# Decoder layer on one core: another cyclic order of all engines' steps

## The chip, the cores and the metric

The kernel runs on one core of a Trainium2 chip. The metric is the device time of one execution in microseconds (us). A core has TensorE (PE, matmuls; PEld is its weight load), VectorE (DVE), ScalarE (ACT) and GpSimd (POOL), which compute, and SyncE (SP), which here issues the DMAs. Each takes its instructions in a fixed order of its own and waits for others on semaphores.

## The reference

64 sequences of 256 tokens with 256 features each, and a context of 120 tokens per sequence, go through one decoder layer in fp32: local attention (16 heads, each token sees three neighbours to either side), cross attention to the context, causal attention, and a feed-forward block whose output is scaled by a factor from a gate.

```python
x = x + local_attn(_layernorm(x))                # window of 7
x = x + cross_attn(_layernorm(x), ctx_1024)      # 16 heads, 120 keys
x = x + ffn(_layernorm(x))
# ffn(h): h = h + causal_attn(rmsnorm(h, n1_w))
#         xf = rmsnorm(h, n2_w)
#         ef = silu(xf @ up_w.T) @ down_w.T          # 1024 hidden
#         return h + ef * sum(ew)                    # ew: top 2 of the gate's softmax
```

## The kernel before

Each sequence is cut into named steps, and five sequences are in flight at once, each in a lane (a set of buffers; `LANES`, line 14). For one sequence the steps are, in the order of the data:

- `load`; then per layer `moments` (VectorE, GpSimd) and `norm` (ScalarE) for the layernorm, and `turn` (TensorE transposes, L790; ScalarE copies them out, L1028). `turn_ctx` (L797) turns the context.
- Local attention: `project_rows` k, v, q (L810, taken out on VectorE at L1327). SP sends keys and values to DRAM and fetches them back as overlapping windows (`send` L703, `fetch` L719); there is one key window and one value window for all lanes. GpSimd multiplies in twelve chunks (`window_times`: six with keys, L630, six with values, L635), VectorE sums each (`window_reduce`, L1361), with `window_max` (L1370 to L1374), `window_exp` (ScalarE, L1081) and `window_sum` (L1379 to L1382) between the halves. Then `turn_out` (L925) and `project_out` (0) (L939, added on VectorE at L1444).
- Cross (layer 1) and causal (layer 2) attention: `project` (layer, q/k/v) (L832, L838), `max` (layer, part) (masks L860, scores L866; VectorE takes the row maxima, L1407), `shift` (L877; L1411) and `place`, two DMAs that put the maxima beside the queries, `scores` (layer, unit) (L888; ScalarE's exponentials L1075; for the causal layer GpSimd's mask L1232), `values` (L911; `normalise` on VectorE), `project_out` (layer).
- Feed-forward: `turn` (3), `gate` (L950), `up` (0) to (3) (L961; tanh on ScalarE L1108, product on VectorE L1460), `down` (L970; L1469), `store`.

`max` and `scores` use TensorE as four tiles of 32 rows, `values` and `gate` as four tiles of 32 columns; all other steps use the whole array. PSUM has 8 banks: `max` and `scores` take a whole half of four, `values` takes two, the others one. A step may not start before the step that had its bank last has been taken out.

The order is made when the program is built, by `Plan` (line 306). TensorE's order is the sorted list of `n + POSITION[step]`, n being the sequence, so one table gives a cyclic order in which each sequence does the same as the one before it one turn later:

```python
if engine == "PE":
    due[i] = POSITION.get((name, args), 0.0)
else:
    due[i] = min((due[j] for j in followers[i]), default=6.0) + SHIFTED.get((name, args, engine), 0.0)
...
line = sorted((n + due[i], n, i) for n, i in todo if parts[i].engine == "PE")
```

Every other engine takes, of the steps whose inputs are there by the planner's durations, the one due first; a step is due when its earliest follower is, shifted by `SHIFTED`. At the two ends of the run (`FILLING`, `LOOKS`) TensorE may look up to 60 entries ahead for a step that is ready. Where the planner expects TensorE to stand still for more than 1 us (`LONG_WAIT`), it puts dummy bf16 matmuls in front of the next step (`passing`; L770), one for each 0.213 us of expected idle time beyond 0.8 us, twice that while it takes TensorE to be cold. Once, at the start, the weights are loaded and derived; on VectorE these are the biases (L1292, L1296) and the scaling of the causal, up, gate and down weights (L1301 to L1305).

Of the kernel before, what the change touches and what calls it, by code (L numbers as in the profile page):

```python
# [29 lines left out]
ACT = mybir.ActivationFunctionType  # L30
# [28 lines left out]
def score_units(layer):  # L59
# [28 lines left out]
POSITION = {("turn", (0,)): -0.0773, ("turn_ctx", ()): -0.0394, ("project_rows", ("k",)): -0.0389, ("project_rows",  # L88
    ("v",)): 0.0516, ("project_rows", ("q",)): 0.0643, ("project", (1, "v")): 0.8052, ("turn_out", ()): 1.0641,
    ("project_out", (0,)): 1.2473, ("project", (1, "k")): 1.2641, ("turn", (1,)): 1.4729, ("project", (1, "q")):  # L90
    1.5195, ("max", (1, 0)): 1.6554, ("max", (1, 1)): 1.6713, ("shift", (1,)): 1.8861, ("scores", (1, 1)): 1.9724,
    ("scores", (1, 0)): 2.0874, ("values", (1,)): 2.3718, ("project_out", (1,)): 2.5298, ("turn", (2,)): 2.6364,
    ("project", (2, "k")): 2.7808, ("project", (2, "q")): 2.8094, ("max", (2, 0)): 2.8523, ("project", (2, "v")):
    2.899, ("max", (2, 1)): 3.0514, ("max", (2, 2)): 3.1338, ("shift", (2,)): 3.2929, ("scores", (2, 1)): 3.4513,
    ("scores", (2, 0)): 3.53, ("scores", (2, 2)): 3.6057, ("values", (2,)): 3.8413, ("project_out", (2,)): 3.9289,
    ("turn", (3,)): 4.2641, ("up", (0,)): 4.3625, ("up", (1,)): 4.3677, ("gate", ()): 4.4232, ("up", (2,)): 4.4727,
    ("up", (3,)): 4.4907, ("down", ()): 4.6197}
# [208 lines left out]
class Plan:  # L306
# [3 lines left out]
    def __init__(self, N, T, C):  # L310
# [14 lines left out]
        for i in reversed(range(len(parts))):  # L325
            name, args, engine = parts[i][:3]
# [4 lines that stand above are left out]
        engines = ("PE", "ACT", "DVE", "POOL", "SP")  # L331
# [1182 lines left out]
```

How the kernel before makes its waits and increments, by code:

```python
        def once(eng, known, what, signal, count):  # L649
            if what not in known:
                known.add(what)
                eng.wait_ge(signal, count)
# [1 line left out]
        def wait_taken(eng, name, n, *args):  # L655
            for b, used in fills[name, n, args]:
                eng.wait_ge(emptied[b], used + 1)
# [2 lines left out]
            @block.sync  # L661
# [19 lines left out]
                                dst = W[what] if dst is None else dst[:, :, 0:E] if what == "gate" else dst  # L681
                                sp.dma_start(dst if what in staged or what == "gate" else dst[:],
                                             src.rearrange("(k p) n -> p k n", p=P)).then_inc(loaded[n], 16)
                    elif name == "zeros":
                        sp.wait_ge(filled_ones, 1)
                        for first in (0, T + HALO):
                            dst = passed_on[:, first:first + HALO, :].rearrange("a r d -> r a d")
# [1 line left out]
                            sp.dma_start(dst, src).then_inc(zeroed, 16)  # L690
                    elif name == "load":
                        before = plan.before["lane", seq, ()]
                        if before:
                            sp.wait_ge(stored[s], reached["stored", "store", before[0], ()])
                        sp.dma_start(x[s][:], t["x"][seq].rearrange("(b p) d -> p b d", p=P)).then_inc(x_loaded[s], 16)
                        sp.dma_start(cx[s][0:C, :], t["ctx_1024"][seq]).then_inc(ctx_loaded[s], 16)
```

## Time and profile before

| | |
|---|---|
| time, median of 3 runs | 3522.82 us (3520.79 to 3526.21) |
| profiled execution, its own time | 3523.18 us |
| its span, first to last instruction | 3521.5 us |
| granted TensorE clock | 0.999 of full |
| TensorE, matmuls | 3464.6 us busy, 98%, 36557 instructions |
| TensorE, weight loads | 2788.9 us, 79% |
| VectorE | 2674.4 us, 76% |
| ScalarE | 1828.8 us, 52% |
| GpSimd | 2498.7 us, 71% |
| DMA | 223.35 MB, mean 63 GB/s |

The busy shares are means over the whole span. Where one engine is near 100% over a stretch, the length of that stretch is read from its own instructions and their starts; where it is not, from what it waits for. TensorE's instructions overlap, so the length of a step is read from start to start and not from its duration. A dummy matmul counts as busy.

### The profile page before, as it was taken

What the parts mean: (1) busy time and instruction counts of PE and PEld (TensorE: products, weight loads), DVE (VectorE), ACT (ScalarE), POOL (GpSimd) and SP (SyncE); (2) the same over time, 40 slices, a digit from 0 to 9 for tenths busy, and PEclk for the clock granted to TensorE, in tenths of its full rate; (3) what the DMA queues carried; (4) which work ended last, traced back from release to release, by engine and by line L of the source; (5) the groups of instructions that cost most, each with busy time, mean ns of one, the idle gap of its engine ahead of it and who ended that gap; (6) DMA issues with size and microseconds to landing.
All of it is one profiled execution on the core that took longest, in us unless ns stands there. A gap on an engine that the chain in (4) does not pass through costs nothing.

```text
span 3521.5 us, 92506 instructions
## 1 busy us (share of the span) xinstructions
PE 3464.6 (98%) x36557; PEld 2788.9 (79%) x36557; DVE 2674.4 (76%) x5867; ACT 1828.8 (52%) x4241; POOL 2498.7 (71%) x3160
## 2 busy tenths in 40 slices
PE   8899999999999999999999999999999999999998
PEld 5577888888888888888888888888888888888876
DVE  5677787787787787787787787787787787787763
ACT  3344555555555555555545545545545545545542
POOL 5767777777777777777777777777777777777731
PEclk9999999999999999999999999999999999999999
DMA  5111221121121121221121221221221121121200
GB/s 182 50 51 50 70 73 51 68 74 51 68 74 52 67 74 50 69 74 50 66 77 47 69 77 46 69 77 47 69 77 47 69 77 47 69 77 47 69 8 10
DMA packets 90151, 223.35 MB, mean 63 GB/s; under 512 B 9286, under 2 KB 56706, under 8 KB 73346
## 3 DMA queue, kind: packets, MB, share of 16 engines
q1 hardware_dynamic: 89730, 217.44, 18.1%
q8 instruction: 300, 4.92, 0.6%
q14 instruction: 121, 0.99, 0.1%
HBM read 164.92 MB, written 50.39 MB: 61 GB/s over the span
## 4 chain that ended last, share of the span: by engine, by line
PE 94%; POOL 2%; ACT 2%; DVE 2%; issue 1%; SPq 0%; DMA 0%; DVEq 0%; POOLq 0%; ACTq 0%
PE ps L970 13%; PE ps L961 13%; PE ps L832 11%; PE ps L810 10%; PE ps L888 9%; PE ps L939 9%; PE ps L866 9%; PE ps L911 8%; PE ps L838 5%; PE ps L790 3%; PE ps L860 1%; PE ps L877 1%; ACT prob L1075 1%; PE ps L925 1%; POOL chunks L635 1%; DVE nmax L1407 1%
## 5 line engine op out<-in xcount | busy, mean ns | idle before, releaser
L635 POOL TENSOR_TENSOR chunks<-v_windows,xT 128x560 f32<-128x560 f32 (+1 forms) x384 | 879.6, 2301 | 92.2 <-DVE xT L1382 89.2
L1407 DVE TENSOR_REDUCE nmax<-ps 128x4 f32<-128x480 f32 (+2 forms) x1280 | 776.9, 671 | 182.8 <-PE ps L866 182.6
L1075 ACT ACTIVATE prob<-ps 128x256 f32<-128x256 f32 (+2 forms) x1536 | 670.7, 556 | 457.7 <-PE ps L888 457.5
L630 POOL TENSOR_TENSOR chunks<-rest,k_windows 128x512 f32<-128x512 f32 (+1 forms) x384 | 552.2, 1455 | 373.9 <-DMA k_windows<-passed_on 301.1
L1361 DVE TENSOR_REDUCE held<-chunks 128x80 f32<-128x560 f32 (+1 forms) x384 | 294.6, 768 | 321.2 <-POOL chunks L635 319.8
L961 PE MATMUL ps<-xT,w_up 128*128 128x256 f32 x2048 | 480.3, 383 | 1.4 <-ACT xT L1028 1.3
L970 PE MATMUL ps<-w_down,held 128*128 128x256 f32 x2048 | 459.1, 382 | 1.1 <-DVE held L1460 1.0
L970 PEld LDWEIGHTS ps<-w_down,held 128*128 128x128 f32 x2048 | 383.8, 190 | 60.1 <-DVE held L1460 2.8
L961 PEld LDWEIGHTS ps<-xT,w_up 128*128 128x128 f32 x2048 | 372.4, 190 | 69.4 <-issue 20.6
L1232 POOL TENSOR_SCALAR_AFFINE_SELECT prob<-prob 128x512 f32<-128x512 f32 x512 | 311.3, 642 | 50.6 <-ACT prob L1075 50.6
L1028 ACT COPY xT<-ps 128x512 f32<-128x512 f32 x256 | 152.9, 597 | 361.6 <-PE ps L790 361.6
L1361 DVE TENSOR_REDUCE xT<-chunks 128x32 f32<-128x512 f32 (+1 forms) x384 | 291.9, 760 | 21.8 <-POOL chunks L630 21.7
L911 PE MATMUL ps<-prob,va 120*32 120x256 f32 (+2 forms) x6144 | 303.5, 346 | 4.2 <-ACT prob L1075 2.0
L911 PEld LDWEIGHTS ps<-prob,va 120*32 120x32 f32 (+1 forms) x6144 | 179.7, 110 | 122.4 <-issue 45.9
L866 PE MATMUL ps<-held 32*128 32x120 f32 (+2 forms) x4096 | 260.2, 321 | 3.2 <-ACT held L1045 2.4
L888 PE MATMUL ps<-held 32*128 32x128 f32 (+2 forms) x3072 | 241.4, 380 | 10.0 <-issue 4.6
L1204 POOL TENSOR_TENSOR x<-x,y 128x512 f32<-128x512 f32 x64 | 81.4, 1272 | 233.8 <-DVE y L1444 233.8
L1016 ACT ACTIVATE held<-x,nmean,rstd 128x256 f32<-128x256 f32 x256 | 140.0, 595 | 186.0 <-POOL nmean L1179 186.0
L1108 ACT ACTIVATE rest<-ps 128x512 f32<-128x512 f32 x256 | 154.7, 604 | 115.9 <-PE ps L961 115.9
L888 PEld LDWEIGHTS ps<-held 32*128 32x128 f32 (+1 forms) x3072 | 123.1, 181 | 97.2 <-issue 90.1
L1460 DVE SCALAR_TENSOR_TENSOR held<-rest,ps 128x512 f32<-128x512 f32 x256 | 172.7, 675 | 23.1 <-ACT rest L1108 22.4
L1418 DVE STREAM_TRANSPOSE ps<-ps 128x512 f32<-128x512 f32 x256 | 170.1, 707 | 20.0 <-PE ps L911 19.3
(152 smaller groups left out, 6783.8 us busy)
## 6 DMA issues: line engine op xcount, KB each, us to landing
k_windows<-passed_on SPq DMA_DIRECT2D x64, 1024.0 KB, 5.0
v_windows<-passed_on SPq DMA_DIRECT2D x64, 1024.0 KB, 5.0
x<-in_x SPq DMA_DIRECT2D x64, 256.0 KB, 2.9
passed_on<-rest SPq DMA_DIRECT2D x64, 256.0 KB, 2.3
passed_on<-held SPq DMA_DIRECT2D x64, 256.0 KB, 3.7
out<-x SPq DMA_DIRECT2D x64, 256.0 KB, 2.2
y<-in_ctx SPq DMA_DIRECT2D x64, 120.0 KB, 2.9
held<-nmaxT SPq DMA_DIRECT2D x256, 8.0 KB
```

The costliest lines, as they stand in the source:

```text
L630: return engine.tensor_tensor(chunk_of(c).rearrange("p (j d) -> p j d", d=D), token_rows["q"][s][:, b, :].unsqueeze(1).to_broadcast([P, n, ...
L635: return engine.tensor_tensor(chunk_of(c).rearrange("p (h i j) -> p h i j", i=HD, j=WINDOW), window("v", b * D + first * HD, (HD, n), (1, ...
L810: last = nc.tensor.matmul(ps[:, b, tb * D:(tb + 1) * D], tokens, W[f"local_{w}"][:, k, :], start=(k == 0), stop=(k == 1))
L832: last = nc.tensor.matmul(ps[:, b, m * n:(m + 1) * n], wt[:, k, m * P:(m + 1) * P], src[:, k, 0:n], start=(k == 0), stop=(k == 1))
L866: last = nc.tensor.matmul(ps[:, to[r], place * keys:(place + 1) * keys], qT[s][e][rows, m, tb * P:(tb + 1) * P], kT[L][s][e][rows, m, 0:keys],
L888: last = nc.tensor.matmul(ps[0:keys, to[r], n * qs:(n + 1) * qs], kT[L][s][e][rows, m, key0:key0 + keys], qT[s][e][rows, m, q0:q0 + qs], s ...
L911: last = nc.tensor.matmul(ps[SLOT * j:SLOT * (j + 1), b, e * T + q0:e * T + q0 + qs], va[s][0:keys, kb, head:head + SLOT], pr[0:keys, j, c ...
L961: last = nc.tensor.matmul(ps[:, b, m * T:(m + 1) * T], w_up[:, k, (2 * m2 + m) * P:(2 * m2 + m + 1) * P], xT[s][:, k, :], start=(k == 0), ...
L970: last = nc.tensor.matmul(ps[:, b, tb * D:(tb + 1) * D], hid[s][:, m, tb * P:(tb + 1) * P], w_down[:, m, :], start=(m == 0), stop=(m == F ...
L1075: last = nc.scalar.activation(prob_pair(seq, L, m)[0:keys, :, r, col:col + qs], of_pair, ACT.Exp, scale=SCALE)
L1361: nc.vector.tensor_reduce(to, chunk_of(c).rearrange("p (x i) -> p x i", i=width), AX_X, ALU.add).then_inc(reduced[s], 1)
L1407: nc.vector.tensor_reduce(of_heads[:, ms[0]:ms[-1] + 1, :, r], src, AX_X, ALU.max, negate=True).then_inc(emptied[b], 1)
```

## The change

The numbers in `POSITION` and `SHIFTED` are others; all else is the same. The number of steps on each engine and all their instructions are the same but for the dummies: 328 before, 248 now. Two entries of the diff:

```diff
-POSITION = {("turn", (0,)): -0.0773, ("turn_ctx", ()): -0.0394, ("project_rows", ("k",)): -0.0389, ("project_rows",
...
+POSITION = {("turn", (0,)): 0.9219, ("turn_ctx", ()): 0.9774, ("project_rows", ("k",)): 0.9776, ("project_rows",
...
-SHIFTED = {("down", (), "DVE"): -0.0629, ("fetch", ("k",), "SP"): 0.2, ("fetch", ("v",), "SP"): 0.5928, ("gate", (),
...
+SHIFTED = {("down", (), "DVE"): 0.325, ("fetch", ("k",), "SP"): -0.274, ("gate", (), "ACT"): 0.1684, ("max", (1, 0),
...
```

TensorE's order over one cycle in the middle of the run, with the sequence that each step belongs to. Before: turn_ctx 30, project_rows k 30, scores (1,1) 28, max (2,1) 27, project_rows v 30, turn_out 29, project_rows q 30, scores (1,0) 28, max (2,2) 27, project_out (0) 29, turn (3) 26, project (1,k) 29, shift (2) 27, up (0) 26, up (1) 26, values (1) 28, gate 26, scores (2,1) 27, up (2) 26, turn (1) 29, up (3) 26, project (1,q) 29, project_out (1) 28, scores (2,0) 27, scores (2,2) 27, down 26, turn (2) 28, max (1,0) 29, max (1,1) 29, project (2,k) 28, project (1,v) 30, project (2,q) 28, values (2) 27, max (2,0) 28, shift (1) 29, project (2,v) 28, turn (0) 31, project_out (2) 27.

Now: turn_ctx 30, project_out (2) 26, project_rows k 30, scores (1,0) 28, max (2,1) 27, project (1,v) 28, turn_out 29, project_rows v 30, max (2,2) 27, scores (1,1) 28, project_rows q 30, shift (2) 27, project_out (0) 29, turn (3) 26, values (1) 28, gate 26, scores (2,1) 27, up (0) 26, up (1) 26, up (2) 26, project_out (1) 28, turn (1) 29, scores (2,0) 27, up (3) 26, project (1,q) 29, down 26, turn (2) 28, scores (2,2) 27, max (1,0) 29, project (2,q) 28, project (2,k) 28, max (1,1) 29, project (1,k) 30, values (2) 27, max (2,0) 28, shift (1) 29, project (2,v) 28, turn (0) 31.

The first place: TensorE from `down` on (L790 is `turn`, L866 `max` (1), L888 with 128x128 `scores` (2,2), L832 and L838 projections, L911 `values` (2)). Before:

```order
L970 MATMUL ps<-w_down,held 128x256 x16
L790 MATMUL ps<-ident,held 128x128 x4
L866 MATMUL ps<-held 128x120 x4
L866 MATMUL ps<-y,held 128x120 x4
...
L832 MATMUL ps<-xT,w_causal_k 128x256 x4
L838 MATMUL ps<-w_cross_v,y 120x256 x2
L832 MATMUL ps<-xT,w_causal_q 128x256 x4
L911 MATMUL ps<-prob,va 32x256 x4
```

Now:

```order
L970 MATMUL ps<-w_down,held 128x256 x16
L790 MATMUL ps<-ident,held 128x128 x4
L888 MATMUL ps<-held 128x128 x4
L888 MATMUL ps<-held,rest 128x128 x4
...
L866 MATMUL ps<-held 128x120 x4
L866 MATMUL ps<-y,held 128x120 x4
...
L832 MATMUL ps<-xT,w_causal_q 128x256 x4
L832 MATMUL ps<-xT,w_causal_k 128x256 x4
L866 MATMUL ps<-held 128x120 x4
L866 MATMUL ps<-y,held 128x120 x4
...
L832 MATMUL ps<-y,w_cross_k 128x120 x4
L911 MATMUL ps<-prob,va 32x256 x4
```

The two `max` (1) steps, 32 matmuls in one run before, are apart, the second between two projections, and the causal `scores` (2,2) stands ahead of the first.

The second place: VectorE in the first sequence, from its fifth window reduce on. Before:

```order
L1361 TENSOR_REDUCE xT<-chunks 128x32
L1398 TENSOR_TENSOR va<-ps,b_cross_v 120x16x16
L1301 TENSOR_SCALAR w_causal_v<-w_causal_v,scale 128x256
...
L1305 TENSOR_SCALAR w_down<-w_down 128x2048
L1361 TENSOR_REDUCE xT<-chunks 128x32
L1327 TENSOR_TENSOR rest<-ps,b_local_q 128x512
L1370 TENSOR_TENSOR xT<-xT,edge_mask 128x224
```

Now:

```order
L1361 TENSOR_REDUCE xT<-chunks 128x32
L1327 TENSOR_TENSOR held<-ps,b_local_v 128x512
L1370 TENSOR_TENSOR xT<-xT,edge_mask 128x224
...
L1382 TENSOR_TENSOR xT<-xT,rsum 128x224
L1301 TENSOR_SCALAR w_causal_v<-w_causal_v,scale 128x256
...
L1305 TENSOR_SCALAR w_down<-w_down 128x2048
L1361 TENSOR_REDUCE held<-chunks 128x96
```

The scaling of the weights has moved from ahead of `window_max` to behind `window_sum`.

The third place: TensorE ahead of the first `turn_out` (L925). Before:

```order
L832 MATMUL ps<-y,w_cross_k 128x120 x4
L810 MATMUL ps<-w_local_q,xT 128x256 x4
L770 MATMUL ps<-ident_b 128x512 x73
L925 MATMUL ps<-ident,held 128x128 x4
L939 MATMUL ps<-w_local_o,xT 128x256 x4
```

Now:

```order
L832 MATMUL ps<-y,w_cross_k 128x120 x4
L838 MATMUL ps<-w_cross_v,y 120x256 x2
L810 MATMUL ps<-w_local_v,xT 128x256 x4
L810 MATMUL ps<-w_local_q,xT 128x256 x4
L770 MATMUL ps<-ident_b 128x512 x61
L925 MATMUL ps<-ident,held 128x128 x4
L939 MATMUL ps<-w_local_o,xT 128x256 x4
```

The dummies are 61 in place of 73, and the last cross-key projection (L832) stands three steps ahead of them where it stood one step ahead. Three earlier places with 10, 4 and 4 dummies, ahead of TensorE's first steps, are gone.

## Rows read from the trace of the kernel before

**Rows 1.** The page: busy us and share of each engine; shares of the chain.
```profile
PE 3464.6 (98%) x36557; PEld 2788.9 (79%) x36557; DVE 2674.4 (76%) x5867; ACT 1828.8 (52%) x4241; POOL 2498.7 (71%) x3160
...
PE 94%; POOL 2%; ACT 2%; DVE 2%; issue 1%; SPq 0%; DMA 0%; DVEq 0%; POOLq 0%; ACTq 0%
```

**Rows 2.** Busy time by stretch: stretch, length, each engine's busy us (instructions), clock, DMA.
```profile
232.00:3147.00 2915.00, 2904.05 (x31126) 2367.55 (x31124) 2284.37 (x5005) 1564.84 (x3626) 2143.00 (x2693) 1.00 0.19 64
```

**Rows 3.** The chain in order of time: start us, us, what.
```profile
2017.18 7.10 PE ps L970 x32
2069.92 7.10 PE ps L970 x32
```

**Rows 4.** TensorE's timeline inside one cycle: start us, us, instructions.
```profile
1677.81 0.30 PE L860 MATMUL ps<-mask_rows,pick_rows 32*128 32x64 bf16 x16 [0.19 <-issue]
...
1687.99 0.71 PE L888 MATMUL ps<-held 32*128 32x256 f32 x8
...
1689.07 1.99 PE L961 MATMUL ps<-xT,w_up 128*128 128x256 f32 x8
1690.90 0.60 PE L790 MATMUL ps<-ident,held 128*128 128x128 f32 x4
...
1693.07 1.89 PE L832 MATMUL ps<-xT,w_cross_q 128*128 128x256 f32 x8
1694.79 1.89 PE L939 MATMUL ps<-w_cross_o,xT 128*128 128x256 f32 x8
1696.61 0.71 PE L888 MATMUL ps<-held 32*128 32x256 f32 x8
...
1697.65 0.50 PE L888 MATMUL ps<-held 32*128 32x128 f32 x8
```

**Rows 5.** Waits, 430 to 3147 us: who waited for whom, us, times, longest.
```profile
POOL chunks L630 <- DMA k_windows<-passed_on: 258.0, 49, 7.3
...
PEld ps L911 <- issue: 34.1, 103, 0.3
```

**Rows 6.** The dummy matmuls of L770 alone, by stretch: PE busy (count) first.
```profile
0.00:72.00 72.00, 23.32 (x91) 9.36 (x91) 0.98 0.60 194
72.00:232.00 160.00, 35.66 (x152) 14.23 (x152) 1.00 0.15 51
...
3434.00:3522.00 88.00, 15.90 (x69) 6.50 (x69) 0.98 0.03 10
```

**Rows 7.** TensorE's timeline, 54 to 84 us.
```profile
55.49 15.92 PE L770 MATMUL ps<-ident_b 128*128 128x512 bf16 x73
71.40 0.66 PE L925 MATMUL ps<-ident,held 128*128 128x128 f32 x4
```

**Rows 8.** GpSimd's timeline, 55 to 76 us.
```profile
57.25 13.32 POOL L635 TENSOR_TENSOR chunks<-v_windows,xT 128x672 f32<-128x672 f32 x6 [11.05 <-DVE xT L1382]
```

**Rows 9.** The timelines of VectorE and of ScalarE, 44 to 58 us.
```profile
46.28 0.34 DVE L1301 TENSOR_SCALAR w_causal_v<-w_causal_v,scale 128x256 f32<-128x256 f32 x1
...
48.42 1.22 DVE L1305 TENSOR_SCALAR w_down<-w_down 128x2048 f32<-128x2048 f32 x1
...
50.75 0.38 DVE L1370 TENSOR_TENSOR xT<-xT,edge_mask 128x224 f32<-128x224 f32 x1
...
55.31 0.40 ACT L1081 ACTIVATE xT<-xT 128x224 f32<-128x224 f32 x1
```

**Rows 10.** Waits of TensorE over the whole run.
```profile
PE ps L970 <- DVE held L1460: 1.0, 2, 0.6
```

**Rows 11.** The timelines of ScalarE and of VectorE inside one cycle.
```profile
1689.21 2.06 ACT L1075 ACTIVATE prob<-ps 128x512 f32<-128x512 f32 x4 [0.86 <-PE ps L888]
1691.14 0.63 ACT L1108 ACTIVATE rest<-ps 128x512 f32<-128x512 f32 x1
...
1693.96 0.69 DVE L1460 SCALAR_TENSOR_TENSOR held<-rest,ps 128x512 f32<-128x512 f32 x1
```

**Rows 12.** TensorE's timeline, 228 to 244 us.
```profile
231.62 0.60 PE L790 MATMUL ps<-ident,held 128*128 128x128 f32 x4
```

More of the change, by code:

```diff
@@ L86 @@
 BEHIND = {("weights", (3,), "SP"): ("fetch", ("k",), "SP", 0), ("weights", (4,), "SP"): ("fetch", ("v",), "SP", 0)}
-POSITION = {("turn", (0,)): -0.0773, ("turn_ctx", ()): -0.0394, ("project_rows", ("k",)): -0.0389, ("project_rows",
[L89 to L97, printed above, removed]
@@ new lines @@
+POSITION = {("turn", (0,)): 0.9219, ("turn_ctx", ()): 0.9774, ("project_rows", ("k",)): 0.9776, ("project_rows",
+    ("v",)): 1.1332, ("project_rows", ("q",)): 1.1518, ("project", (1, "k")): 1.8134, ("turn_out", ()): 2.0879,
+    ("project_out", (0,)): 2.1783, ("turn", (1,)): 2.2808, ("project", (1, "q")): 2.4795, ("max", (1, 0)): 2.7336,
+    ("max", (1, 1)): 2.7883, ("shift", (1,)): 2.9153, ("scores", (1, 0)): 3.0592, ("project", (1, "v")): 3.0877,
+    ("scores", (1, 1)): 3.1516, ("values", (1,)): 3.1832, ("project_out", (1,)): 3.2808, ("turn", (2,)): 3.6475,
+    ("project", (2, "q")): 3.7881, ("project", (2, "k")): 3.7881, ("max", (2, 0)): 3.9003, ("project", (2, "v")):
+    3.9219, ("max", (2, 1)): 4.0874, ("max", (2, 2)): 4.1511, ("shift", (2,)): 4.1766, ("scores", (2, 1)): 4.2144,
+    ("scores", (2, 0)): 4.4344, ("scores", (2, 2)): 4.6983, ("values", (2,)): 4.8138, ("project_out", (2,)): 4.9776,
+    ("turn", (3,)): 5.1785, ("gate", ()): 5.1834, ("up", (0,)): 5.2155, ("up", (1,)): 5.2297, ("up", (2,)): 5.2301,
+    ("up", (3,)): 5.4346, ("down", ()): 5.4797}
```

50 lines of the change are left out of this document (25 added, 25 removed).

## The prediction

> **What bounds the kernel now.** I read the page's busy shares and its chain first. TensorE is busy 3464.6 of 3521.5 us (98%), VectorE 76%, GpSimd 71%, ScalarE 52%, and TensorE holds 94% of the chain that ended last [rows 1]. So time counts where TensorE works longer or waits. The busy sums by stretch come next: from 232 to 3147 us it is busy 2904 of 2915 us [rows 2], so its empty time lies in the filling before and in the drain behind. In the chain, `down` of one sequence starts at 2017.18 and of the next at 2069.92 [rows 3]: one cycle is some 52.7 us. Two levers follow: the length of a cycle, paid about 57 times, and the empty time at the two ends, paid once.
>
> TensorE's timeline shows what order costs inside a cycle [rows 4]. A projection with whole-array neighbours goes from start to start in 1.72 us (1693.07 to 1694.79). The same work right ahead of a group of 32-row tiles takes 1.82 (1694.79 to 1696.61), right behind such a group 1.83 (1689.07 to 1690.90). I call a run of `max`, `scores`, `values` and `gate` steps between whole-array steps a spell. A spell costs its neighbours 0.10 each, 0.20 together, and its own last step 0.04 more: `scores` takes 1.04 with another `scores` behind it (1696.61 to 1697.65) and 1.08 with `up` behind it (1687.99 to 1689.07). The waits list has the same from the weight loader: 103 pauses ahead of L911 with 34.1 us together, 0.33 each [rows 5], two a cycle.
>
> The empty time shows in the dummy matmuls of L770, which stand where the planner expects TensorE to wait for over 1 us: 91 of them before 72 us, 152 from there to 232 us, 69 behind 3434 us [rows 6]. Of the 73 ahead of sequence 0's `turn_out` one takes 15.92/73 = 0.218 us [rows 7].
>
> **The change part by part.** No instruction changes its form, tile or size; the positions and the orders that hang on them do.
>
> *1. Spells.* Before, a cycle has six: scores/max, scores/max, values/gate/scores, scores/scores, max/max, values/max. Changed, `scores` (2,0) stands alone between `turn` and `up`, `scores` (2,2) has joined `max` (1,0), and `max` (1,1) stands alone between two projections: seven. Counted over the whole orders, 398 spells become 455, 57 more. At 0.20 + 0.04 = 0.24 us each that is **+13.7 us**, all on TensorE, where nothing hides it. Lower end: the neighbours alone at 0.19, +10.8. Upper end: a spell that also shows a pause such as the 0.19 us ahead of L860 at 1677.81 [rows 4], 0.43, +24. I take 0.24, a difference of like rows.
>
> The Trainium skill (TensorEngine Tiling, Key Properties) says that a change of the tiling mode drains the array. Its page TensorE: Matmul & The Clock Gate (Single matmul latency) puts a drain at about 175 ns; by that, an estimate, the 114 added switches would cost 20 us. The trace shows such a cost on both sides of a spell, but 0.10 each.
>
> *2. The first sequence.* GpSimd starts the value half of sequence 0 at 57.25, after 11.05 us without work, on the end of VectorE's softmax sum [rows 8]. On VectorE the scaling of the weights, 46.28 to 49.64, stands ahead of L1370 at 50.75; on ScalarE the exponential (L1081) at 55.31 stands behind four evictions of cross keys [rows 9], the last fed by the projection two steps ahead of the dummies. The change puts the scaling behind the softmax sum, so L1370 comes 3.3 us earlier, and the feeding projection four steps ahead of the dummies, two more projections earlier. GpSimd's six products end at 57.25 + 13.32 = 70.57 [rows 8] and `turn_out` starts at 71.40 [rows 7]; sequence 1's products queue behind them, so what is won here shifts the whole filling. I take **-5.0 us**. The 12 dummies fewer in front of `turn_out`, 61 for 73, say 2.6 of it, with projections drawn forward; the 18 dummies that the first 30 us lose stood in waits for loads, which stay, and count nothing. Ends: -1.7 (the exponential moves by one projection) and -6.7 (scaling, and two projections). Against it stands that SP fetches sequence 0's keys behind two more sends; no row prices that, and it lies inside these ends.
>
> *3. The rest of the filling.* From `project_out` of sequence 0 to `turn` of sequence 5 there are 119 dummies for 152 [rows 6]. 33 x 0.218 = **-7.2 us**, if the planner's expectation is as good as for the 73, whose last ended when `turn_out` could start. Ends -3 and -10.
>
> *4. The drain.* The last four places (19, 11, 19, 4) are alike. Ahead of them 27 dummies become 15: at 15.90/69 = 0.23 [rows 6] **-2.8 us**; ends 0 and -4.
>
> *5. Waits in the cycle.* Now GpSimd waits 258.0 us in 49 pauses for the key window [rows 5], and its jitter comes through to TensorE's `scores` and `max` groups. In the changed order seven steps in place of four stand between the key and the query projection, so the keys are there when the queries come and GpSimd starts on the queries: I take off 0.2 us a cycle. Against that, `project` (2,q) takes the first bank of `scores` (2,2) 0.9 us after that step, where it stood behind ScalarE's first two of eight activations, and `turn_out` a bank of `max` (2,1) 1 us behind it: 0.1 each, 0.25 with smaller ones, from distances between starts. Net 0.05 x 57 = **+3 us**; ends -10 (the gain alone) and +14 (the loss alone).
>
> Sum: 13.7 - 5.0 - 7.2 - 2.8 + 3 = +1.7 on the profiled execution's own 3523.18: 3524.9, rounded to **3525 us**. The median before, 3522.82, lies 0.4 below that execution. A measurement of this kernel tells about 0.2% (7 us) from no change; the forecast is inside.
>
> **The rivals.**
>
> *A. The ends win (faster).* Parts 2 to 4 come out at their good ends, -6.7 - 10 - 4 = -20.7, spells at +10.8, and of part 5 half the gain, -5: 3523.2 - 14.9 = **3508**. For it: fewer dummies in three separate places. Against it: it needs all of them.
>
> *B. `down` waits for `up` (3) (slower).* Now a cross-query projection, `project_out` (1) and two `scores` lie between them, and L970 waited for L1460 only twice [rows 10]. Changed, only the projection is left. From the end of the lone `scores` (2,0) to `down` TensorE has `up` (3) and that projection, 1.83 + 1.72 = 3.55 us; in them ScalarE has four exponentials, 2.06, and the tanh, 0.63, and VectorE the product, 0.69 [rows 11]: 3.38. The slack is 0.17 us, and the case decides from there; VectorE's window softmax (L1370 to L1374) stands right ahead of that product and can use it up. 0.5 us late is 57 x 0.5 = 28 us, **3553**. Against it: each piece fits, just.
>
> *C. A switch costs more than its like rows say.* If an added switch costs TensorE half of the weight loader's pause [rows 5], 0.17, and not 0.12, then 114 x 0.17 = 19 stand in place of 13.7: **3531**, at the edge of slower. The Trainium skill's two pages named above would have it so; the trace agrees that a switch costs something and shows less of it.
>
> *D. The switches cost nothing more,* since TensorE would wait there for its banks anyway: parts 2 to 5 alone, 3523.2 - 12 = **3511**. Rows 4 speak against it. It goes with A.
>
> **How the numbers follow.** The forecast, 3516 to 3530, has 0.38. Faster: A and D 0.33. Slower: B 0.14, C 0.08, other new waits of part 5's kind 0.07, together 0.29. The range takes in A and a little below, and reaches to B: 3503 to 3552. The likeliest case's own is 3516 to 3530.
>
> **What would show it.** (1) `down` every 52.9 to 53.2 us in the middle of the run; at 52.7 or less part 1 is wrong, over 53.4 B or part 5 is. (2) The `up` behind the lone `scores` (2,0), and the projections around the lone `max` (1,1), 0.1 us longer than with whole-array neighbours. (3) `turn_out` of sequence 0 at 65 to 67 us and `turn` of sequence 5 near 219, now 231.62 [rows 12]. (4) For B, a wait of L970 for L1460 in every cycle. (5) GpSimd's wait for the key window mostly gone, one for the query rows in its place. The wrong sign in (3), or a cycle over 53.4, makes the prediction wrong.

## The result, and the profile after

The changed kernel takes **3559.27 us**, median of 4 runs (3554.51 to 3565.55), against 3524.11 (3520.79 to 3526.21) for the kernel before beside it: ratio 1.0102, 95% interval 1.0090 to 1.0114, so 35 us slower. The prediction said 3525 within 3503 to 3552; the result lies outside. The profiled execution took 3554.51, at the low end of the four, with a span of 3552.8.

The page of the changed kernel, its busy times and its chain:

```profile
PE 3458.9 (97%) x36477; PEld 2781.3 (78%) x36477; DVE 2740.6 (77%) x5867; ACT 1815.3 (51%) x4241; POOL 2502.5 (70%) x3160
...
PE 85%; DMA 7%; DVE 2%; POOL 2%; ACT 1%; issue 1%; SPq 1%; DVEq 0%; POOLq 0%; ACTq 0%
```

TensorE has 94% of the chain in [rows 1] and 85% here; DMA, at 0% before, has 7%. The busy times by stretch, first the stretch of [rows 2], then the dummies of L770 alone in the first stretch of [rows 6]:

```profile
232.00:3147.00 2915.00, 2876.98 (x30772) 2337.10 (x30771) 2316.50 (x4943) 1532.47 (x3578) 2116.44 (x2656) 1.00 0.19 64
...
0.00:72.00 72.00, 11.74 (x42) 4.80 (x43) 0.93 0.66 204
```

TensorE is empty for 38 us of the 2915 in which it was empty for 11. So the loss is in the cycle and not at the ends. The starts of `down` in the three traces say how much of it; the third column is the first experiment below.

| | before | changed | placing first |
|---|---|---|---|
| `down` of sequence 3 starts | 375.3 | 372.3 | 366.4 |
| `down` of sequence 58 starts | 3286.0 | 3317.9 | 3282.0 |
| mean cycle between them (55) | 52.92 | 53.56 | 53.01 |
| shortest cycle | 52.7 | 52.8 | 52.8 |
| from there to the end of the span | 235.5 | 234.9 | 235.0 |
| span | 3521.5 | 3552.8 | 3517.0 |

The filling gained 3 us, the drain half a us, and 55 cycles lost 0.63 each, 35. The shortest cycle hardly grew: most of the loss comes in some cycles and not in others. The waits from 430 to 3147 us, as in [rows 5], name the reason:

```profile
POOL chunks L630 <- DVE rest L1327: 328.5, 47, 7.1
...
PE ps L888 <- DMA held<-nmaxT: 31.0, 35, 2.3
```

The last row is new. `scores` waits for the two DMAs of `place`, which put the row maxima beside the queries; over the whole run TensorE waits 36.4 us for them, 39 times. The chain of one such cycle, in order of time:

```profile
2171.75 4.56 DMA passed_on<-held
2176.33 0.32 SPq L719
2176.70 0.54 SPq L728
2177.28 3.99 DMA held<-nmaxT
2181.32 1.15 PE ps L888 x16
```

Read upwards: causal `scores` (2,1) starts at 2181.32, when the maxima have landed. SP issued them at 2176.70 (L728), right behind the 1 MB fetch of the value windows (L719). The fetch had waited for the send of the value rows, on its way since 2171.75. The times of issue in the kernel before, and what a fetch takes from issue to landing, the median on the page of before:

```profile
1677.99 0.32 SPq L719 DMA_DIRECT2D v_windows<-passed_on  x1
...
1683.94 1.10 SPq L728 DMA_DIRECT2D held<-nmaxT  x2
...
v_windows<-passed_on SPq DMA_DIRECT2D x64, 1024.0 KB, 5.0
```

Changed, VectorE's eviction of the maxima and TensorE around the same place:

```profile
2175.66 0.40 DVE L1411 COPY nmaxT<-ps 16x256 f32<-16x256 f32 x1
...
2179.16 0.41 PE L950 MATMUL ps<-xT,w_gate 128*32 128x64 f32 x16
2181.32 0.71 PE L888 MATMUL ps<-held 32*128 32x256 f32 x8 [1.74 <-DMA held<-nmaxT]
```

Before, the fetch left 5.95 us ahead of the placing, so it was over by the median of 5.0, and `scores` began 4.05 us behind the placing (1687.99 in [rows 4]) without a wait. Changed, the fetch leaves 0.37 us ahead of it, since `project_rows` v, whose result SP sends and fetches back, stands four steps ahead of `shift` (2) where it stood eight (5.84 us from start to start, 9.75 before); and TensorE wants the maxima sooner, since only `project_out`, `turn`, `values` and `gate` are left between `shift` and `scores`. Over sequences 8 to 57 the fetch leads by 3.2 to 6.0 us before and by 0.36 to 2.32 changed. Sorted by that lead, the time from placing to `scores` in the changed kernel is:

| lead of the fetch, us | cycles | placing to `scores`, mean (least to most) |
|---|---|---|
| 0.36 | 9 | 4.61 (4.36 to 5.05) |
| 0.5 to 1 | 7 | 4.42 (3.90 to 5.27) |
| 1 to 1.5 | 20 | 3.84 (3.42 to 4.47) |
| 1.5 to 2.32 | 14 | 3.49 (3.42 to 4.05) |

3.42 is what TensorE's own steps take, the case without a wait. In the first rows lead and time add up to nearly the same. In the 29 of these 50 cycles in which `scores` waits for over 0.3 us, it starts 5.12 us behind the issue of the fetch in the mean (4.72 to 6.11), whatever the lead, and the fetch itself takes 5.0 in the median: the placing, small as it is, lands about when the 1 MB does. What inside the transfers makes it so, no run here shows. An estimate from these numbers: there is hardly a wait where the fetch leads by 5.1 - 3.4 = 1.7 us or more.

### The profile page after: what moved, and what is told of

It reads as the page before. It is cut to its first block, busy times and chain, and to the rows that moved or that the text cites. A ratio compares the mean times of both kernels' runs of the same rounds, so it can differ in the third digit from the quotient of the medians.

```text
span 3552.8 us, 92347 instructions
## 1 busy us (share of the span) xinstructions
PE 3458.9 (97%) x36477; PEld 2781.3 (78%) x36477; DVE 2740.6 (77%) x5867; ACT 1815.3 (51%) x4241; POOL 2502.5 (70%) x3160
## 4 chain that ended last, share of the span: by engine, by line
PE 85%; DMA 7%; DVE 2%; POOL 2%; ACT 1%; issue 1%; SPq 1%; DVEq 0%; POOLq 0%; ACTq 0%
PE ps L961 13%; PE ps L970 12%; PE ps L832 11%; PE ps L888 9%; PE ps L810 9%; PE ps L866 8%; PE ps L939 7%; PE ps L911 6%; PE ps L838 5%; DMA held<-nmaxT 4%; PE ps L790 2%; DMA passed_on<-held 1%; PE ps L860 1%; PE ps L770 1%; DVE nmax L1407 1%
## 5 line engine op out<-in xcount | busy, mean ns | idle before, releaser
L635 POOL TENSOR_TENSOR chunks<-v_windows,xT 128x560 f32<-128x560 f32 (+1 forms) x384 | 872.0, 2295 | 31.0 <-DVE xT L1382 25.5
L1028 ACT COPY xT<-ps 128x512 f32<-128x512 f32 x256 | 150.2, 587 | 658.2 <-PE ps L790 658.2
L961 PEld LDWEIGHTS ps<-xT,w_up 128*128 128x128 f32 x2048 | 380.0, 191 | 90.5 <-issue 41.2
L911 PE MATMUL ps<-prob,va 120*32 120x256 f32 (+2 forms) x6144 | 303.5, 346 | 1.5 <-POOL prob L1232 0.9
L888 PE MATMUL ps<-held 32*128 32x128 f32 (+2 forms) x3072 | 236.2, 377 | 39.7 <-DMA held<-nmaxT 36.4
L866 PE MATMUL ps<-held 32*128 32x120 f32 (+2 forms) x4096 | 254.9, 318 | 1.7 <-ACT held L1045 1.6
L911 PEld LDWEIGHTS ps<-prob,va 120*32 120x32 f32 (+1 forms) x6144 | 180.0, 110 | 96.3 <-issue 13.8
L888 PEld LDWEIGHTS ps<-held 32*128 32x128 f32 (+1 forms) x3072 | 121.0, 181 | 103.2 <-issue 49.6
L1316 DVE BATCH_NORM_STATS2 stats<-x 128x6 f32<-128x256 f32 x384 | 143.8, 416 | 68.4 <-DMA x<-in_x 66.3
L866 PEld LDWEIGHTS ps<-held 32*128 32x128 f32 x4096 | 163.5, 186 | 23.8 <-issue 22.1
```

The lines of the kernel that those rows point to most:

```text
L635: return engine.tensor_tensor(chunk_of(c).rearrange("p (h i j) -> p h i j", i=HD, j=WINDOW), window("v", b * D + first * HD, (HD, n), (1, ...
L866: last = nc.tensor.matmul(ps[:, to[r], place * keys:(place + 1) * keys], qT[s][e][rows, m, tb * P:(tb + 1) * P], kT[L][s][e][rows, m, 0:keys],
L888: last = nc.tensor.matmul(ps[0:keys, to[r], n * qs:(n + 1) * qs], kT[L][s][e][rows, m, key0:key0 + keys], qT[s][e][rows, m, q0:q0 + qs], s ...
L911: last = nc.tensor.matmul(ps[SLOT * j:SLOT * (j + 1), b, e * T + q0:e * T + q0 + qs], va[s][0:keys, kb, head:head + SLOT], pr[0:keys, j, c ...
L961: last = nc.tensor.matmul(ps[:, b, m * T:(m + 1) * T], w_up[:, k, (2 * m2 + m) * P:(2 * m2 + m + 1) * P], xT[s][:, k, :], start=(k == 0), ...
```

## The experiments

Theory P: the placing is late because it is issued behind the 1 MB fetch. Rivals: L, its latency alone is too long for the new order; S, the added spells are the loss; and for the filling, D and G on the dummies. Each edit is made after the orders are planned, unless a position is changed. The kernel before ran beside each (3522.53, 3523.52 and 3523.92 us in the three groups).

**1. The placing ahead of the fetch in SP's queue.**

```diff
+        sp = self.order["SP"]
+        for j in range(len(sp) - 1):
+            if sp[j][0] == "fetch" and sp[j][2] == ("v",) and sp[j + 1][0] == "place" and sp[j + 1][2] == (CAUSAL,):
+                sp[j:j + 2] = sp[j + 1], sp[j]
```

> The changed kernel with one exchange in SP's queue: wherever the fetch of the value windows (1 MB) stands right ahead of the placing of the causal maxima, place (2), the placing now goes first. Everything else keeps its order. Theory P (placing behind the fetch): TensorE's wait of scores (2,1) for nmaxT, 36 us over the run and some 29 us by the stretched distance gate to scores, comes from the placing's transfer standing behind the 1 MB fetch issued 0.36 to 2.3 us before it. Then this wait goes (under 5 us in all) and the time is 3527 to 3534, take 3530. Theory L (the placing's own latency is too long for the 4.2 us that the changed TensorE order leaves): the wait stays and the time is 3553 to 3560. Theory S (the 57 added spells are the loss, as part 1 of the prediction priced them at 13.7 us, and more): at most 10 us better, 3549 to 3559.

Measured: **3516.70 us** (3514.99 to 3518.75), ratio to before 0.998 (0.9971 to 0.9989). SP's queue and TensorE in one cycle (L723, L732 and L892 are L719, L728 and L888 of the changed kernel), and the busy times of the stretch:

```profile
2152.23 1.10 SPq L732 DMA_DIRECT2D held<-nmaxT  x2
2153.43 0.38 SPq L723 DMA_DIRECT2D v_windows<-passed_on  x1
...
2155.65 0.71 PE L892 MATMUL ps<-held 32*128 32x256 f32 x8
...
232.00:3147.00 2915.00, 2911.17 (x31124) 2367.92 (x31124) 2331.46 (x5003) 1554.29 (x3630) 2140.72 (x2695) 1.00 0.19 64
```

The wait for the maxima has left the waits list, and TensorE is empty for 4 us of the stretch. P holds; L and S fall: the same TensorE order, with the same latency and all its spells, is 43 us faster than the changed kernel by the medians (36 by the profiled spans, the changed kernel's being its fastest run) and 5.8 us faster than the kernel before. The gain is above the 29 us expected, and the time 10 us under the range given for P. By the profiled spans the 36 us gained are the 36.4 us of waiting; the expectation had counted 29 of them. That the changed kernel's other runs, 3 to 11 us longer, wait more is likely but not shown, since only one of them has a trace.

**2. The kernel before, its fetch held back until the maxima are ready.**

```diff
+                        if w == "v" and later and later[0][0] == "place" and later[0][2] == (CAUSAL,):
+                            wait_taken(sp, "shift", later[0][1], CAUSAL)
```

> The kernel before, with its own TensorE order and six spells a cycle; SP now holds the fetch of the value windows back until the causal maxima are ready to be placed, so that the fetch leaves some 0.4 us ahead of place (2) and not 3.2 to 6.0 us. Theory P: the placing lands 4.5 to 5.3 us after its issue as in the changed kernel, while TensorE leaves it 4.05 us: 0.5 to 1.3 us of waiting a cycle at scores (2,1), a wait of L888 for nmaxT of 30 to 70 us appears that the kernel before did not have, and the time is 3550 to 3595, take 3570. Theory L: 4.05 us are enough for the placing whatever stands before it, no such wait, 3520 to 3532 (a few us for a later fetch). Should GpSimd come to wait for v_windows instead, the later fetch is the cause and not the placing; the waits list tells.

Measured: **3597.04 us** (3592.31 to 3598.72), ratio 1.0213 (1.0196 to 1.0230), 74.5 us slower. The wait over the run (L891 is L888):

```profile
PE ps L891 <- DMA held<-nmaxT: 63.7, 58, 2.6
```

The lead is 0.36 us in every cycle, and `scores` starts 4.31 to 5.31 us behind the placing in every cycle, mean 4.71, as in the first line of the table, or 5.07 behind the fetch. The wait appears in the old order, in 58 pauses. P holds; the time is 2 us above the range given. GpSimd waits once, 9.5 us, for the value windows, in the filling; that belongs to the later fetch itself.

**3. The fetch in halves, one ahead of the placing and one behind.**

```diff
-                        sp.dma_start(windows[w][:], ...)
+                            half_fetch(s, 0)
+                            if later and later[0][0] == "place" and later[0][2] == (CAUSAL,):
+                                held_back.append(s)
+                            else:
+                                half_fetch(s, 1)
```

> The changed kernel with each value fetch in two transfers of 512 KB; where place (2) follows, the first half goes ahead of it and the second behind it. Theory P with the bytes ahead as what counts: the placing waits for about half as long, which the slack of about 0.6 us between 3.4 and 4.0 us largely covers; the wait of scores (2,1) falls from 36 us to 3 to 15 us, time 3532 to 3545. Theory P with the mere presence of a large transfer ahead as what counts: the wait stays near 30 us, 3553 to 3562. Theory L: no change, 3555 to 3562.

Measured: 3521.78 us (3519.10 to 3524.45), ratio 0.9999 (0.9990 to 1.0009). Over the run (L907 is L888):

```profile
PE ps L907 <- DMA held<-nmaxT: 9.9, 16, 1.2
```

Half the bytes ahead leave 9.9 of 36.4 us of waiting, as P expects where bytes count; 5 us over experiment 1, below the range of 3532 to 3545, which had been laid too high with the same 29 us. In the cycles that wait, `scores` starts 3.85 us behind the half fetch, for 5.12 behind the whole one. This kernel still has the placing behind a fetch that waits for its send; so that blocking, without the second half, costs at most these 9.9 us.

**4. Fewer dummies ahead of the first `turn_out`.**

```diff
+        self.passing["turn_out", 0, ()] -= 28
```

> The changed kernel with 33 dummy matmuls ahead of turn_out of sequence 0 in place of 61, nothing else changed. In the changed kernel they start at 60.26 us, behind 7.6 us without work, and end at 76.3, though the last reduce that turn_out waits for is done by about 69. So turn_out should start at 69 to 70 us. Theory D (the dummies delay the filling as a whole): everything behind comes 6 to 7 us earlier, 3552. Theory G (GpSimd, whose products of sequence 1 began at 69.2 regardless, sets the filling): turn (3) of sequence 1 and down of sequence 0 move by less than 3 us, time 3556 to 3560.

Measured: **3567.08 us** (3564.83 to 3571.37), 8 slower than the changed kernel. The filling did what it should: `turn_out` of sequence 0 starts at 68.96 for 76.16, and `down` of sequence 0 at 203.6 for 208.8. That is 5.2 of the 6 to 7 us of D at the start; G, under 3 us there, falls. At `down` of sequence 3, 369.0 for 372.3, 3.3 us are left. From there to `down` of 58 a cycle takes 53.92 us in place of 53.56. TensorE waits 48.8 us for the maxima (36.4), and the granted clock fell more often. The fetch leads by only 0.36 us in 15 of the 50 cycles of the table, where it was 9: the start of the run has a say in which cycles that happens. Both theories gave a time that leaves the cycles as they were, 3552 and 3556 to 3560, and both missed; the loss in the cycles was in neither.

**5. One spell more in the kernel before.**

```diff
-    ("project_out", (0,)): 1.2473, ... ("max", (1, 0)): 1.6554, ("max", (1, 1)): 1.6713,
+    ("project_out", (0,)): 1.2473, ... ("max", (1, 0)): 1.6280, ("max", (1, 1)): 1.6713,
```

> The kernel before with one step moved: max (1,0) stands ahead of turn (2) and not behind it, so max (1,0) and max (1,1) are two spells; 398 spells become 456, 58 more, and the order is otherwise the same. This prices a spell by itself. Theory S24 (part 1 of the prediction, 0.24 us a spell on TensorE with nothing to hide it): 58 x 0.24 = 14 us, 3536 against 3522.5. Theory S9 (with the placing out of the way the changed order's cycle was 53.01 us against 52.92, so that the added spell costs 0.09): 5 us, 3528. If the step's new place makes a wait for banks or for xT of turn (2), the waits list shows it.

Measured: **3590.55 us** (3589.22 to 3592.53), ratio 1.0191 (1.0177 to 1.0205): a miss for both. The waits from 430 to 3147 us, and ScalarE and TensorE behind one `down`:

```profile
PE ps L866 <- DVE nmax L1407: 50.7, 51, 1.2
...
2386.63 0.59 ACT L1028 COPY xT<-ps 128x512 f32<-128x512 f32 x1 [3.61 <-PE ps L790]
...
2387.58 0.50 PE L866 MATMUL ps<-held 32*128 32x120 f32 x8 [0.98 <-DVE nmax L1407]
```

`max` (1,1) now waits 1.0 us in every cycle. The list puts that down to VectorE's maxima, but by the kernel's plan the four banks of `max` (1,1) were last those of `down`, `turn` (2) and `scores` (2,0), none of them of a `max`. `turn` (2) now stands right ahead of `max` (1,1), without `max` (1,0) between, and ScalarE takes it out from 2386.63 to 2387.22 (L1028); `max` (1,1) starts 0.36 us behind that, as it starts 0.35 us behind the same copy in the kernel before. So the wait is for ScalarE's copy. The mean cycle is 54.08 for 52.92: 1.16, of which 1.0 is this wait. The experiment prices a bank wait, and leaves some 0.2 for the spell.

**6. The changed kernel with `scores` (2,1) one step later.**

```diff
-    ("scores", (2, 1)): 4.2144
+    ("scores", (2, 1)): 4.2200
```

> The changed kernel with SP's queue as it was, the 1 MB fetch ahead of place (2), but scores (2,1) one step later on TensorE: behind up (0) and not behind gate. The placing then has 1.8 us more, some 5.2 us from its issue. Price: scores (2,1) is a spell of its own, 59 more. Theory P (the placing lands 4.3 to 5.3 us after its issue behind the fetch, and only lateness counts): the wait of L888 for nmaxT is nearly gone (under 5 us), and the time is that of the run with the placing first, 3516.7, plus 59 spells: 3522 at 0.09, 3531 at 0.24. Rival (the fetch's traffic slows more than this one wait): 3540 or more with the wait gone.

Measured: **3611.49 us** (3609.36 to 3612.34), ratio 1.0250 (1.0236 to 1.0264). TensorE's waits, 430 to 3147 us:

```profile
PE ps L970 <- DVE held L1460: 38.9, 49, 0.9
```

The wait for the maxima is gone (0.2 us), as P says, and in its place `down` waits for `up` (3) in 49 of some 51 cycles: rival B of the prediction, which did not show in the changed kernel (0.6 us in one pause). The planner also moved ScalarE's and VectorE's steps with this edit, and the cycle is 54.5 us. P's 3522 to 3531 were far too low. The time is where the rival put it, 3540 or more with the wait gone, but the new wait is on VectorE and not on the fetch's traffic, so that the experiment says nothing for the rival. It is shown that B's slack is thin, not how much of the 52 us over the changed kernel is B's.

**7. The two `max` (1) together again, placing first.**

```diff
-    ("max", (1, 1)): 2.7883
+    ("max", (1, 1)): 2.7340
```

> The placing first, and max (1,1) back beside max (1,0): 396 spells as before the change (398). Theory S24: 59 spells fewer, 14 us off 3516.7, 3503. Theory S9: 5 us off, 3511. Rival B2 (the spell was split because three groups of four banks in a row, scores (2,2), max (1,0), max (1,1), must wait for ScalarE's eight activations): TensorE waits 0.5 to 1.5 us a cycle ahead of max (1,1), L866 waits for ScalarE's prob, 3540 to 3600.

Measured: **3598.52 us** (3597.00 to 3599.28), ratio 1.0213 (1.0199 to 1.0227), 82 over experiment 1. TensorE between `max` (1,0) and `max` (1,1), L870:

```profile
2394.12 0.82 PE L774 MATMUL ps<-ident_b 128*128 128x512 bf16 x3
2395.62 0.50 PE L870 MATMUL ps<-held 32*128 32x120 f32 x8 [0.67 <-ACT prob L1079]
```

From 2394.12 to 2395.62 TensorE does nothing of use: the third group of four banks in a row waits for ScalarE's exponentials. B2 holds, at the top of its range. The spell that I booked as a pure cost of the change buys these 1.5 us (net 1.25: the mean cycle is 54.26 here and 53.01 in experiment 1).

**8. Placing first and 33 dummies.** Edits 1 and 4 together.

> The placing first and 33 dummy matmuls ahead of turn_out of sequence 0 in place of 61. With 33 and the fetch first, down of sequence 3 came 3.3 us earlier (369.0 for 372.3) but the whole took 8 us longer, with 12 us more waiting for nmaxT and six stretches of lower granted clock. Theory D2 (the start gains 3 to 4 us, and the loss behind it was all in waits for the placing): 3512 to 3514. Rival (fewer dummies cost something else later): 3517 or more.

Measured: **3515.08 us** (3512.61 to 3517.83), ratio to before 0.9977 (0.9967 to 0.9986), the fastest of all, though 1.6 from experiment 1 is within what the runs scatter. TensorE's start (L775 is L770):

```profile
59.02 8.95 PE L775 MATMUL ps<-ident_b 128*128 128x512 bf16 x33 [7.67 <-DVE rest L1332]
```

`turn_out` starts at 68.10, and no wait for the maxima is left. `down` of sequence 3 starts at 359.6 for 366.4, 6.9 earlier; the span ends 3.6 earlier, since a cycle here takes 53.07 us for 53.01. The start gained more than the 3 to 4 us of D2, the end less: the time lies between the ranges of D2 (up to 3514) and of its rival (from 3517) and decides for neither.

**9. `gate` as a spell of its own, placing first.**

```diff
-    ("gate", ()): 5.1834
+    ("gate", ()): 5.2200
```

> The changed kernel with the placing first, and gate one step later, behind up (0): values and scores (2,1) stay together, gate is a spell of its own, 514 spells for 455. It takes one bank only and its followers on VectorE and ScalarE are short, so that no new wait for banks is expected. Theory S24 (a spell costs 0.24 us): 59 x 0.24 = 14 us over 3516.7, 3531. Theory S9: 59 x 0.09 = 5 us, 3522. Rival (scores (2,1) now comes 0.4 us sooner after the placing and waits): a wait of L888 for nmaxT shows, 3535 or more.

Measured: **3538.06 us** (3534.98 to 3539.63), ratio 1.0039 (1.0027 to 1.0052), 21 over experiment 1. TensorE has no wait for the maxima (its weight loader 1.4 us) and no other new wait. TensorE's timeline, from `values` to behind `up` (L965), where experiment 1 has the three `up` together:

```profile
2324.98 1.93 PE L915 MATMUL ps<-prob,va 120*32 120x256 f32 x32
...
2327.92 1.99 PE L965 MATMUL ps<-xT,w_up 128*128 128x256 f32 x8
2329.84 0.43 PE L954 MATMUL ps<-xT,w_gate 128*32 128x64 f32 x16
2330.20 3.72 PE L965 MATMUL ps<-xT,w_up 128*128 128x256 f32 x16
2333.76 1.89 PE L943 MATMUL ps<-w_cross_o,xT 128*128 128x256 f32 x8
```

Experiment 1 for comparison:

```profile
2153.56 1.93 PE L915 MATMUL ps<-prob,va 120*32 120x256 f32 x32
...
2156.72 5.45 PE L965 MATMUL ps<-xT,w_up 128*128 128x256 f32 x24
2162.01 1.89 PE L943 MATMUL ps<-w_cross_o,xT 128*128 128x256 f32 x8
```

`gate` and the three `up` take 0.34 + 5.29 = 5.63 in experiment 1 and 1.92 + 0.36 + 3.56 = 5.84 here: the added spell costs 0.21 us. `values` and `scores` take 2.94 from 2324.98 to 2327.92, where `values`, `gate` and `scores` take 3.16 from 2153.56 to 2156.72 there: less `gate`'s 0.34 that is 2.82, so 0.12 more where a step in row tiles and not one in column tiles follows. Together 0.33, and the cycle is 53.32 for 53.01. S9 is wrong. S24 is nearer, but the spell costs 0.31 to 0.33 us for its 0.24, and its 3531 was 7 us short. An added spell is two added switches of the tiling, 0.16 us each here.

**10. The placing issued from ScalarE's DMA queue.** The fetch leaves SP at the same place as in the changed kernel.

```diff
+        for step in [step for step in self.order["SP"] if step[0] == "place" and step[2] == (CAUSAL,)]:
+            self.order["SP"].remove(step)
+            shift = at_pe["shift", step[1], (CAUSAL,)]
+            act.insert(next((j for j, a in enumerate(act) if at_pe.get(a, -1) > shift), len(act)), step)
```

> The changed kernel with every place (2) issued from ScalarE's DMA queue in place of SP's, at the same moment in the cycle; the 1 MB fetch leaves SP as before. Theory Q (what delays the placing is its place behind the fetch in the same queue): the wait of scores (2,1) for nmaxT falls under 5 us, 3515 to 3522. Theory E (the engines and the memory are shared, whichever queue issues): the wait stays at 20 to 36 us, 3540 to 3560. Both should lose SP's own blocking, where the fetch waits for its send and the placing behind it. ScalarE may pay for the issues: if its waits grow, the time is higher with the wait for nmaxT gone.

Measured: 3554.63 us (3552.14 to 3563.59), ratio 1.0093 (1.0078 to 1.0107). One cycle (L725 the fetch, L1036 the placing, L894 `scores`), and the wait over the run:

```profile
2173.23 0.32 SPq L725 DMA_DIRECT2D v_windows<-passed_on  x1
...
2174.48 1.12 ACTq L1036 DMA_DIRECT2D held<-nmaxT  x2
...
2179.01 0.71 PE L894 MATMUL ps<-held 32*128 32x256 f32 x8 [1.05 <-DMA held<-nmaxT]
...
PE ps L894 <- DMA held<-nmaxT: 35.6, 39, 2.1
```

35.6 us for 36.4: another queue helps nothing. At the same lead the time from placing to `scores` is the same too, 4.32 for 4.42 at 0.5 to 1 us and 3.81 for 3.84 at 1 to 1.5. In 5 of the 50 cycles the first of the two DMAs leaves 0.12 to 0.62 us ahead of the fetch, and `scores` still starts 5.1 to 5.6 us behind it; in experiment 1, where both are issued before the fetch, it is 3.42. Theory E holds, and SP's own blocking, gone here, was worth about 1 us of waiting and at most 5 us of time.

The Trainium skill (DMA: Bandwidth & Descriptors, Issuing engines are not separate DMA queues) says that transfers started by different engines run on the same 16 DMA engines and interleave; the trace agrees, with 35.6 against 36.4 us. The same page of the Trainium skill (Queues, rings and completion order) says that each DMA engine takes turns between the queues, packet by packet. From that one might infer that the 8 KB of a placing in a queue of its own pass the 1 MB; the skill does not say so, and no such gain shows here.

**12. The kernel before with the exchange of experiment 1.** (There is no 11.)

> The kernel before with the same exchange in SP's queue as brought the changed kernel from 3559 to 3517: place (2) ahead of the fetch of the value windows. Here TensorE never waited for nmaxT, so theory P expects nothing: 3519 to 3526, or a loss where the fetch, now some 4.5 us later, makes GpSimd wait for v_windows. Rival (a later fetch is good for something else, such as the other transfers): 3510 to 3517, as in the changed kernel, whose gain over the kernel before would then come from the exchange and not from the order.

Measured: 3532.21 us (3529.18 to 3535.07), ratio 1.0022 (1.0012 to 1.0032), 8.3 slower. Waits over the run (L639 is L635):

```profile
POOL chunks L639 <- DMA v_windows<-passed_on: 11.1, 1, 11.1
```

The cycle is unchanged, 52.96 for 52.92. The loss is in the filling: GpSimd waits for one late fetch until 210.4, TensorE stands still for 4.6 us until 214.4, its granted clock is 0.50 for the 6.8 us from 213.7 on, and `down` of sequence 3 starts at 384.6 for 375.3. So the exchange is no gain by itself, and the 5.8 us by which experiment 1 beats the kernel before belong to the changed order.

## Why the prediction was wrong

Its sum was 1.7 us over the profiled execution of before; with the placing out of the way the changed order comes to 3517.0 - 3521.5 = 4.5 us under it in span. The step that failed is the count of what the change moves: **SP's queue and the DMAs were never part of it**. Part 5, *Waits in the cycle*, looked for what comes late next among banks, GpSimd and ScalarE, and of SP the whole prediction names only the fetch of sequence 0's keys, in part 2. The order of SP's steps in a cycle is the same in both kernels, and that was taken for no change; what changed is the time between them. Rows for it were at hand before: a fetch 3.2 to 6.0 us ahead of a placing, and `scores` 4.05 us behind. The order shows the value rows moved four steps towards `shift` (2), and TensorE's steps from `shift` to `scores` cut. That a placing lands about with the fetch ahead of it, the price of the collision, stood in no row of before. The result also fails two of the prediction's own signs: a cycle over 53.4 us (53.56), and the sign of (3) at `turn_out`.

Part by part:

- *1, spells, +13.7.* Right in mechanism, and in price where it can be read most plainly, around the lone `scores` (2,0) of the changed kernel:

```profile
2189.40 0.60 PE L790 MATMUL ps<-ident,held 128*128 128x128 f32 x4
2189.93 0.71 PE L888 MATMUL ps<-held 32*128 32x256 f32 x8
...
2191.01 1.99 PE L961 MATMUL ps<-xT,w_up 128*128 128x256 f32 x8
2192.84 1.89 PE L832 MATMUL ps<-xT,w_cross_q 128*128 128x256 f32 x8
```

  `turn` takes 0.53 from start to start for 0.44 ([rows 4], 1690.90 to 1691.34), `scores` 1.08 for 1.04, `up` (3) 1.83 and the projection behind it 1.73 for 1.72: 0.24 in all, as predicted. But not all spells are alike. The lone `gate` of experiment 9 costs 0.33, of which 0.12 is `values` with `scores` behind it and not `gate`; and the lone `max` (1,1) saves 1.2 us a cycle of waiting for banks (54.26 in experiment 7, 53.01 in experiment 1).
- *2, the first sequence, -5.0.* Wrong sign on the profiled execution: `turn_out` at 76.16 for 71.40, where 65 to 67 was predicted. GpSimd's value half does start 5.6 us earlier, at 51.66 for 57.25 [rows 8]. Three things undo it. The first two, in the timelines of GpSimd and of VectorE:

```profile
51.66 4.94 POOL L635 TENSOR_TENSOR chunks<-v_windows,xT 128x672 f32<-128x672 f32 x2 [7.72 <-DVE xT L1382]
59.69 8.71 POOL L635 TENSOR_TENSOR chunks<-v_windows,xT 128x560 f32<-128x560 f32 x4 [3.08 <-DVE held L1361]
...
51.67 3.01 DVE L1304 TENSOR_SCALAR w_up<-w_up,scale 128x1024 f32<-128x1024 f32 x1
54.60 2.04 DVE L1304 TENSOR_SCALAR w_gate<-w_gate,scale 128x32 f32<-128x32 f32 x1
...
58.77 0.84 DVE L1361 TENSOR_REDUCE held<-chunks 128x96 f32<-128x672 f32 x1
59.53 0.67 DVE L1327 TENSOR_TENSOR rest<-ps,b_local_q 128x512 f32<-128x512 f32 x1
```

  The scaling of the weights, moved from ahead of the softmax to behind it, now stands ahead of the first reduce and of the eviction L1327. It also takes longer there: 7.4 us, 51.41 to 58.84, for 3.4 in [rows 9]. The two scalings shown ran beside GpSimd's first two products and ended about when these did; before, with GpSimd idle, they took 0.75 and 0.24. GpSimd waits 3.1 us for the reduce, and TensorE's dummies 7.6 us for the bank of the eviction:

```profile
60.26 16.06 PE L770 MATMUL ps<-ident_b 128*128 128x512 bf16 x61 [7.62 <-DVE rest L1327]
76.16 0.60 PE L925 MATMUL ps<-ident,held 128*128 128x128 f32 x4
```

  A string of dummies is a fixed number of matmuls: started late it ends late. The third thing is the clock. While TensorE stood still the granted clock fell, and it is 0.50 from 55.57 to 65.81; so the first 5.6 us of the string ran at half speed (14 dummies), which gives up 2.8 us and takes back the 2.6 that 12 dummies fewer should save: 61 take 16.06 us where 73 took 15.92 [rows 7]. The string starts 4.8 us later than before, at 60.26 for 55.49, and `turn_out` follows. With 33 of them `turn_out` started at 68.10 (experiment 8).
- *3, the rest of the filling, -7.2.* `turn` (0) of sequence 5, predicted near 219, starts at 229.2 for 231.62 [rows 12]; without the surplus dummies and the wait for the placing (experiment 8), at 221.7. Most of the gain was there, behind the two obstacles.
- *4, the drain, -2.8.* 0.5 came.
- *5, waits in the cycle, +3.* Two signs. GpSimd's wait for the keys fell from 258.0 to 28.7 us and one for the query rows (328.5) took its place, as predicted. And the gain beyond the placing was larger than booked: experiment 1's cycle is 0.09 us over that of before, where spells and part 5 said 0.29. The missing term is the placing, 0.55 us a cycle (53.56 to 53.01), 30 us in 55.

Of the rivals, B had the right kind, a new wait in the cycle, and nearly the right price (3553), but at another place and for a DMA; that the number is close is luck. D falls: the switches do cost time. C, 0.17 us a switch, falls for the lone `scores` (0.12 by the rows above), but experiment 9's spell comes to 0.16 a switch. So neither price holds for every spell.

## What to carry to other kernels

When an order is changed, list for every small, urgent DMA what large transfer leaves just ahead of it and how long before, even where the issuing queue keeps its order, and count the small one as landing with the large one: here a lead of 0.4 us and not 5 made a placing of 8 KB transfers over 1 us late. Issue the urgent one first; another issuing queue did not help. And judge a change of order by its parts on the chip: the same TensorE order was 35 us slower or 6 us faster than before by the order of two neighbouring entries in SP's queue, once a cycle. Last, where a step waits for several banks, look up in the plan whose they were before you believe the engine that the waits list names (experiment 5).

## What the runs showed of the hardware

A short wait can cost TensorE its clock as well, and some of VectorE's instructions take longer beside GpSimd's: 3.01 us for 0.75 in part 2 above, and 3.03 at the same place in experiment 8. No experiment takes the two apart. The rest is on the clock. The changed kernel's busy time and granted clock (third number from the right) around a pause of 1.79 us:

```profile
2760.00:2767.00 7.00, 7.00 (x85) 1.00 0.74 239
2767.17:2768.96 1.79, 0.00 (x1) 1.00 0.54 224
2768.96:2770.00 1.04, 1.04 (x12) 0.60 0.00 0
2770.00:2771.00 1.00, 1.00 (x13) 0.50 0.00 0
2772.00:2773.00 1.00, 1.00 (x5) 0.71 0.00 0
```

TensorE had worked without a gap, stood still for 1.79 us, and then ran for 3.4 us (2769.16 to 2772.58) at 0.50 of its clock, the lower level of 1.2 GHz, which costs half of that, 1.7 us; this cycle took 56.3 us. The length of the pause does not decide it alone: the pause of 1.74 at 2181.32 left the clock at 1.00, and so did one of 2.34 us that ended at 739.0. Of 11 pauses over 1.5 us between 300 and 3200 us, two were followed by a fall. In stretches of 50 us from 200 us on, the changed kernel has 2 with a clock under 0.99, experiment 4 has 7, and before and experiment 1 none. Each of these falls begins in, or within 1.5 us behind, a pause ahead of `scores`, of 1.79 to 2.72 us. Experiment 2, whose 58 pauses are mostly shorter, has one, behind its pause of 2.57 us. So fewer dummies at the start made experiment 4 slower by way of longer waits and a lower clock up to thousands of microseconds later: behind `down` of sequence 3 it waits 11 us more for the maxima than the changed kernel (44.5 for 33.3), and its clock falls five times for once, 7 us more, of the 20 that its 55 cycles lose.
